# Weight differences over three tiles a chunk, earlier stores of B's pieces, another order of the first chunks, and 128-row low-rank products

## The chip, the cores and the metric

One core of a Trainium2 chip runs the kernel alone. The metric is the device time of one execution in microseconds (us), as the median of the runs of one kernel; lower is better.

## The reference

`x` has 32 sequences of 128 rows and 2048 columns, all in fp32. Each sequence has an adapter number between 6 and 15. The result adds to `x` a linear layer with bias and the low-rank product of the sequence's adapter:

```
result = einsum('bsd,od->bso', x, base_weight) + base_bias     # 2048 x 2048 weights
A, Bw  = lora_A_w[adapter_ids], lora_B_w[adapter_ids]          # rank 16, 32 adapters
h      = einsum('bsd,brd->bsr', x, A)
out    = x + result + einsum('bsr,bor->bso', h, Bw)
```

## The kernel before, in words

**Splitting.** Every fp32 operand is split into a rounded part (hi) and a rest (lo), and a product is three products: hi with hi, lo with hi, hi with lo. ScalarE writes the hi part (`x_high` L544, `w_high` L549), VectorE the lo part (`x_low` L646, `w_low` L651).

**Phases.** The large product is done with seven half-size products in place of eight (the Strassen-Winograd scheme). The seven are the phases P1, P2, P6, P5, P4, P7, P3, in this order. A phase has 16 tiles of 128 rows; a tile has 8 chunks (k) of 128 input columns, and its sums lie in one of two PSUM accumulators, `acc[0]` and `acc[1]`, by turns. Tile number 2i+j of a phase is `Tile(ph, i, j)`; `place` counts the tiles through all phases (P1 has places 0 to 15, P2 has 16 to 31). The first two tiles are written out apart: TensorE takes chunk 0 of both, then chunk 1 of both, and so on, since weights still arrive (L928 to L934).

**Weight differences.** P6, P5, P4 and P7 use differences of blocks of the weights. They are made during P1. For each of 8 chunks, SyncE loads four blocks of 512 KB into the buffers 2 to 5 of `pool` (`prep_load`, L457), GpSimd makes four subtractions (`prep`, L795), and SyncE stores all four to `w_sums` in DRAM (`prep_store`, L463). Chunk i is loaded in the tile (i, 1) and stored one step later.

**B's pieces.** The matrices B of all adapters are split too, in 8 pieces of 512 KB. Piece n is loaded to buffer 6 (`load_piece`), ScalarE and VectorE write its two parts to `b_stack` (`piece_high`, `piece_low`, both in a tile with j = 1), and `store_piece` (L370) writes three times 512 KB of stacked rows to `b_stacks` in DRAM. Piece 0 is the bias, which `spread_bias` copies to all adapters. Pieces 0 to 4 are made in P1, 5 to 8 in P6. The store of a piece stands in the tile pair behind the one that splits it, and `piece_high` of the next piece waits until it has landed.

**Low-rank part.** h of a sequence is a by-product of P1/P2 and P5/P4 (32 more columns of the weights). In P2, P4, P7 and P3, each tile ends with `turn` (L890: a product of `h_cols` with the unit matrix turns h, 50 rows come out) and `low_rank` (L898: these 50 rows of `h_stack` with the 50 rows of `b_stack`: three stacks of 16 and two of bias). TensorE does both inside the next tile, behind its chunks 1 and 2.

**Queues.** Each engine runs a fixed list in order. SyncE (SP) issues every DMA: its list is the function `step` (L468), called for each place in turn. A wait in it holds up all that stands behind it. In `step(place p)` the x block of tile p+2 is loaded (`load_x`, L298), then A's rows (`load_a`), the block to be added (`load_out`), then the weight blocks, pieces and stores in the order of the function. VectorE's step for place p-1 makes the lo part of tile p and reads out tile p-2; TensorE's tile p waits for both.

Of the kernel before, what the change touches and what calls it, by code (L numbers as in the profile page):

```python
# [19 lines left out]
P = 128  # L20
# [4 lines left out]
RANK = 16  # L25
# [36 lines left out]
PREP_AT = (2, 3, 4, 5)  # L62
BUFFERS = 7

# [45 lines left out]
def loads_before(ph):  # L110

    n = [0] * BUFFERS
    for q in range(ph):
        n[0] += PAIRS
        n[1] += PAIRS
        if q == P1:
            for b in PREP_AT:
                n[b] += PAIRS
# [9 lines left out]
def stores_before(ph):  # L128
    n = [0] * BUFFERS
    for q in range(ph):  # L130
        if q == P1:
            for b in PREP_AT:
                n[b] += PAIRS
# [43 lines left out]

def lora_kernel(nc, xT, x, wT, bias, aT, bT, ids, w_sums, s_sums, u4, bias_rows, b_stacks, out):
# [3 lines left out]
    with ctx:  # L182
# [25 lines left out]
        h_cols = at("h_cols", [P, AC + AC], f32r)  # L208
# [35 lines left out]
        bias_spread = sem("bias_spread")  # L244
        out_added = sem("out_added")
# [42 lines left out]
        def _(sp):  # L288
# [53 lines left out]
            def load_b(tile):  # L342
# [99 lines left out]
            def load_w_first(ph):  # L442

                if ph == P6:
                    for b in PREP_AT:
                        sp.wait_ge(pool_out[b], DMA * PAIRS)
# [10 lines left out]
            def prep_load(i):  # L457
                for b, (half, k) in zip(PREP_AT, ((0, 0), (1, 0), (1, KC), (0, KC))):
                    if not (isinstance(i, int) and i == 0):
                        sp.wait_ge(pool_out[b], DMA * i)  # L460
                    sp.dma_start(pool[:, b], wT[half, bass.ds(k + i, 1)]).then_inc(pool_in[b], DMA)  # L461

            def prep_store(i):  # L463
                sp.wait_ge(w_summed, 4 * i + 4)
                for b, which in zip(PREP_AT, (1, 3, 0, 2)):
                    sp.dma_start(w_sums[which, bass.ds(i, 1)], pool[:, b]).then_inc(pool_out[b], DMA)  # L466

            def step(tile):  # L468
# [7 lines left out]
                if ph == P1 and j == 1:  # L476
                    prep_load(i)
# [57 lines left out]
        def _(act):  # L535
# [38 lines left out]
            def h_high(tile):  # L574
# [8 lines left out]
                nc.scalar.activation(h_cols[:].rearrange("p (c r) -> p c r", c=2)[:, :, 0:RANK],  # L583
                                     h.to_broadcast([P, 2, RANK]), COPY).then_inc(h_hi_done, 1)

            def h_out(tile):
# [4 lines left out]
                nc.scalar.activation(h_stack[0:COLS_B], turned[0:COLS_B, 0:ROWS], COPY).then_inc(h_ready, 1)  # L591
# [202 lines left out]
        def _(gp):  # L794
            def prep(i):  # L795

                b11, b12, b22, b21 = PREP_AT
                for b in PREP_AT:
                    gp.wait_ge(pool_in[b], DMA * (i + 1))
                for n, (to, one, two) in enumerate(((b11, b12, b11), (b12, b22, b12), (b22, b22, b11),  # L800
                                                    (b21, b21, b22))):
                    if n:
                        gp.wait_ge(w_summed, 4 * i + n)
                    nc.gpsimd.tensor_tensor(pool[:, to], pool[:, one], pool[:, two],  # L804
                                            ALU.subtract).then_inc(w_summed, 1)
# [18 lines left out]
            def step(tile):  # L824
# [6 lines left out]
                if ph == P1 and j == 1:  # L831
                    prep(i)
# [19 lines left out]
        def _(pe):  # L852
# [37 lines left out]
            def turn(tile):  # L890
# [4 lines left out]
                nc.tensor.matmul(turned[0:COLS_B, 0:ROWS], h_cols[:, 0:COLS_B], eye[:],  # L895
# [88 lines left out]
```

## Time and profile before

| what | us |
|---|---|
| median of 3 runs (1439.85 to 1442.17) | 1441.3 |
| the profiled execution's own time | 1439.74 |
| its span, first to last instruction | 1437.5 |

The span holds the work of all engines; 2.2 us of the execution's time lie around it. TensorE is busy for 1358.2 us of the span, VectorE for 592.6, GpSimd for 255.9, ScalarE for 222.2. In the views PE is TensorE's matmuls, PEld its weight loads, DVE VectorE, ACT ScalarE, POOL GpSimd, SPq SyncE's queue. PEclk and "clock" are the granted TensorE clock: 1.00 or 9 in tenths is 2.4 GHz, and a mean in between is a stretch that was partly at 1.2 GHz. A group in the timeline starts at the first number and takes the second; `[idle before <-releaser]` says how long its engine had stood idle and what ended that.

### The profile page before, as it was taken

How to read it: one execution, taken by the hardware profiler on the slowest of the kernel's cores; microseconds unless marked ns; L12 is line 12 of the kernel's file. 1: busy time of each engine (PE TensorE's matmuls, PEld its weight loads, DVE VectorE, ACT ScalarE, POOL GpSimd, SP SyncE). 2: the span in 40 equal slices, each digit the busy share in tenths (PEclk: the TensorE clock that was granted, in tenths of full speed). 3: DMA queues.
4: the chain of work that ended last, by engine and by line, in shares of the span. 5: the costliest groups of instructions: out<-in, count | busy, mean ns of one | idle time of the engine just before them, and what ended most of it. 6: DMA issues, size and time to landing. Idle time of an engine off the chain costs nothing.

```text
span 1437.5 us, 18259 instructions
## 1 busy us (share of the span) xinstructions
PE 1358.2 (94%) x7136; PEld 1212.2 (84%) x7136; DVE 592.6 (41%) x807; ACT 222.2 (15%) x408; POOL 255.9 (18%) x121
## 2 busy tenths in 40 slices
PE   7899677599999999899999999999999999999998
PEld 7899676499999787779999999999977777777776
DVE  4532233544445544444333464333544444522222
ACT  4010011111112211112111121101211111211110
POOL 1522233421221000002444432221100000000000
PEclk9999888699999999999999999999999999999999
DMA  7566565744455887786666883334467768855552
GB/s 241 181 229 219 208 252 188 269 154 154 151 204 200 290 288 261 285 291 244 252 225 224 293 281 100 115 116 174 159 204 232 232 232 290 290 188 190 192 192 99
DMA packets 93513, 308.78 MB, mean 215 GB/s; under 512 B 10482, under 2 KB 19746, under 8 KB 93474
## 3 DMA queue, kind: packets, MB, share of 16 engines
q1 hardware_dynamic: 93474, 308.35, 61.7%
q8 instruction: 14, 0.23, 0.1%
q14 instruction: 25, 0.20, 0.0%
HBM read 211.82 MB, written 97.01 MB: 215 GB/s over the span
## 4 chain that ended last, share of the span: by engine, by line
PE 71%; DMA 11%; SPq 8%; POOL 5%; DVE 2%; issue 2%; ACT 0%; POOLq 0%; DVEq 0%
PE acc L859 25%; PE acc L872 22%; PE acc L865 20%; POOL pool L804 5%; DMA s_sums<-pool 5%; DMA pool<-wT 4%; PE acc L906 3%; SPq L466 1%; SPq L378 1%; SPq L461 1%; DMA w_raw<-wT 1%; SPq L309 1%; SPq L320 1%; SPq L290 1%; DMA pool<-xT 1%
## 5 line engine op out<-in xcount | busy, mean ns | idle before, releaser
L872 PE MATMUL acc<-w_lo,x_hi 128*128 128x352 f32 (+2 forms) x2304 | 571.5, 347 | 6.8 <-DVE w_lo L651 6.8
L872 PEld LDWEIGHTS acc<-w_lo,x_hi 128*128 128x128 f32 x2304 | 408.7, 191 | 41.2 <-DVE w_lo L651 7.4
L859 PE MATMUL acc<-w_hi,x_hi 128*128 128x352 f32 x1536 | 344.4, 333 | 59.1 <-DVE keep L728 40.8
L859 PE MATMUL acc<-w_hi,x_lo 128*128 128x352 f32 x1536 | 336.3, 327 | 0.0
L859 PEld LDWEIGHTS acc<-w_hi,x_hi 128*128 128x128 f32 x1536 | 261.4, 193 | 68.0 <-issue 48.7
L859 PEld LDWEIGHTS acc<-w_hi,x_lo 128*128 128x128 f32 x1536 | 268.6, 192 | 0.0
L865 PE MATMUL acc<-w_hi,x_hi 128*128 128x512 f32 x768 | 246.3, 401 | 5.2 <-DVE x_lo L646 5.1
L865 PE MATMUL acc<-w_hi,x_lo 128*128 128x512 f32 x768 | 241.0, 394 | 0.0
L646 DVE TENSOR_TENSOR x_lo<-pool,x_hi 128x1024 fp32r<-128x1024 f32 x110 | 146.7, 1334 | 204.6 <-ACT x_hi L544 204.6
L544 ACT ACTIVATE x_hi<-pool 128x1024 fp32r<-128x1024 f32 x110 | 116.1, 1056 | 682.7 <-PE acc L872 354.1
L815 POOL TENSOR_TENSOR pool<-pool,keep 128x1024 f32<-128x1024 f32 x48 | 120.5, 2526 | 434.8 <-DMA pool<-x 434.8
L865 PEld LDWEIGHTS acc<-w_hi,x_hi 128*128 128x128 f32 x768 | 139.3, 189 | 50.7 <-issue 9.8
L734 DVE TENSOR_TENSOR pool<-acc,pool 128x352 f32<-128x352 f32 (+2 forms) x176 | 102.2, 631 | 181.8 <-PE acc L906 181.8
L865 PEld LDWEIGHTS acc<-w_hi,x_lo 128*128 128x128 f32 x768 | 144.8, 189 | 33.7
L804 POOL TENSOR_TENSOR pool<-pool 128x1024 f32<-128x1024 f32 x32 | 87.6, 2737 | 184.1 <-DMA pool<-wT 182.2
L651 DVE TENSOR_TENSOR w_lo<-w_raw,w_hi 128x1024 fp32r<-128x1024 f32 x56 | 77.2, 1393 | 41.7 <-ACT w_hi L549 41.3
L690 DVE TENSOR_TENSOR h_sum<-acc,h_part 128x32 f32<-128x32 f32 x32 | 6.1, 192 | 165.7 <-PE acc L872 165.7
L659 DVE TENSOR_TENSOR w_hi<-a_raw,w_hi 128x64 fp32r<-128x64 f32 (+1 forms) x96 | 66.8, 722 | 2.3 <-ACT w_hi L562 2.3
L549 ACT ACTIVATE w_hi<-w_raw 128x1024 fp32r<-128x1024 f32 x56 | 58.2, 1051 | 52.4 <-DMA w_raw<-wT 36.0
L583 ACT ACTIVATE h_cols<-h_keep 128x32 fp32r<-128x32 f32 x64 | 14.3, 223 | 306.8 <-DVE h_keep L693 306.8
L906 PE MATMUL acc<-b_stack,h_stack 50*128 50x512 f32 (+2 forms) x160 | 46.5, 386 | 2.8 <-ACT h_stack L591 2.8
L706 DVE TENSOR_TENSOR keep<-acc,keep 128x1024 f32<-128x1024 f32 x16 | 19.6, 1224 | 67.1 <-PE acc L872 67.1
(29 smaller groups left out, 344.3 us busy)
## 6 DMA issues: line engine op xcount, KB each, us to landing
pool<-xT SPq DMA_DIRECT2D x142, 512.0 KB, 5.8
pool<-x SPq DMA_DIRECT2D x64, 512.0 KB, 5.4
out<-pool SPq DMA_DIRECT2D x48, 512.0 KB, 2.8
pool<-wT SPq DMA_DIRECT2D x32, 512.0 KB, 8.0
w_sums<-pool SPq DMA_DIRECT2D x32, 512.0 KB, 4.0
w_raw<-w_sums SPq DMA_DIRECT2D x32, 512.0 KB, 6.1
s_sums<-pool SPq DMA_DIRECT2D x32, 512.0 KB, 8.8
pool<-s_sums SPq DMA_DIRECT2D x32, 512.0 KB, 5.5
```

What stands on the lines that cost most here:

```text
L544: nc.scalar.activation(x_hi[:, j], x_raw(j), COPY).then_inc(x_hi_done, 1)
L549: nc.scalar.activation(w_hi[:, s, AC:AC + HALF], w_raw[:, s], COPY).then_inc(w_hi_done, 1)
L646: nc.vector.tensor_tensor(x_lo[:, j], x_raw(j), x_hi[:, j], ALU.subtract).then_inc(x_lo_done, 1)
L651: nc.vector.tensor_tensor(w_lo[:, s], w_raw[:, s], w_hi[:, s, AC:AC + HALF], ALU.subtract).then_inc(w_lo_done, 1)
L659: did = nc.vector.tensor_tensor(w_hi[:, s:s + m, hi + RANK:hi + AC], a_raw[:, j, k:k + m], w_hi[:, s:s + m, hi:hi + RANK], ALU.subtract)
L734: did = nc.vector.tensor_tensor(rows, sums, rows, ALU.add)
L804: nc.gpsimd.tensor_tensor(pool[:, to], pool[:, one], pool[:, two], ALU.subtract).then_inc(w_summed, 1)
L815: did = nc.gpsimd.tensor_tensor(to, pool[:, b], kept, ALU.add)
L859: mm = nc.tensor.matmul(acc[j][:, o, 0:COLS_A], xs, w_hi[:, s, base + o * COLS_A:base + (o + 1) * COLS_A], start=(k == 0 and part == 0), s ...
L865: mm = nc.tensor.matmul(acc[j][:, o], xs, w_hi[:, s, AC + o * BANK:AC + (o + 1) * BANK], start=(k == 0 and part == 0), stop=False)
L872: mm = nc.tensor.matmul(acc[j][:, o, low:low + n], x_hi[:, j, k], w_lo[:, slot(ph, k), first:first + n], start=False, stop=end and (ph not ...
L906: mm = nc.tensor.matmul(acc[j][:, o, low:low + m], h_stack[0:COLS_B], b_stack[0:COLS_B, j, first:first + m], start=False, stop=True, skip_ ...
```

## The change

Five things. The differences are made with three buffers (2, 3, 4): three loads, three subtractions and three stores, and then one load, one subtraction and one store in buffer 2 again. A chunk is spread over three tiles (places 4+3n, 5+3n, 6+3n), so that the work runs from place 4 to place 27, into P2. A piece of B is stored in the tile that splits it (j = 1). The first two tiles share their chunks 0 to 4 only; then tile 0 does its last three chunks, then tile 1. `h_cols` has 128 columns, zero beyond the 50, and `turn` and `low_rank` work on 128 rows; for this GpSimd clears the rows of `b_stack` once in P1 and once in P6 (`clear_b`), and the first `load_b` of P2 and of P4 waits for it.

```diff
-PREP_AT = (2, 3, 4, 5)
+PREP_AT = (2, 3, 4)
+PREP_FROM = 4
+FIRST_CHUNKS = [(j, k) for k in range(5) for j in range(2)] + [(j, k) for j in range(2) for k in range(5, KC)]
...
+def prep_at(tile):
+    n, part = divmod(place(tile) - PREP_FROM, 3)
+    return (n, part) if 0 <= n < KC else (None, None)
...
-        h_cols = at("h_cols", [P, AC + AC], f32r)
+        h_cols = at("h_cols", [P, P], f32r)
...
-                if n < 2:
-                    sp.wait_ge(piece_out, DMA * (2 + 3 * 4))
-                elif ph == P4 and i == 0:
-                    sp.wait_ge(piece_out, DMA * (2 + 3 * 8))
+                if i == 0 and ph in (P2, P4):
+                    sp.wait_ge(b_cleared, 1 if ph == P2 else 2)
...
-            def prep_load(i):
-                for b, (half, k) in zip(PREP_AT, ((0, 0), (1, 0), (1, KC), (0, KC))):
-                    if not (isinstance(i, int) and i == 0):
-                        sp.wait_ge(pool_out[b], DMA * i)
-                    sp.dma_start(pool[:, b], wT[half, bass.ds(k + i, 1)]).then_inc(pool_in[b], DMA)
-
-            def prep_store(i):
-                sp.wait_ge(w_summed, 4 * i + 4)
-                for b, which in zip(PREP_AT, (1, 3, 0, 2)):
-                    sp.dma_start(w_sums[which, bass.ds(i, 1)], pool[:, b]).then_inc(pool_out[b], DMA)
+            def prep_load(n):
+                a, b, c = PREP_AT
+                if n:
+                    sp.wait_ge(pool_out[a], DMA * 2 * n)
+                    sp.wait_ge(pool_out[b], DMA * n)
+                    sp.wait_ge(pool_out[c], DMA * n)
+                for at, what in ((a, wT[0, n]), (b, wT[1, n]), (c, wT[1, KC + n])):
+                    sp.dma_start(pool[:, at], what).then_inc(pool_in[at], DMA)
+
+            def prep_store(n):
+                a, b, c = PREP_AT
+                sp.wait_ge(w_summed, 4 * n + 3)
+                for at, which in ((a, 1), (b, 3), (c, 0)):
+                    sp.dma_start(w_sums[which, n], pool[:, at]).then_inc(pool_out[at], DMA)
+
+            def prep_load_last(n):
+                a = PREP_AT[0]
+                sp.wait_ge(pool_out[a], DMA * (2 * n + 1))
+                sp.dma_start(pool[:, a], wT[0, KC + n]).then_inc(pool_in[a], DMA)
+
+            def prep_store_last(n):
+                a = PREP_AT[0]
+                sp.wait_ge(w_summed, 4 * n + 4)
+                sp.dma_start(w_sums[2, n], pool[:, a]).then_inc(pool_out[a], DMA)
...
-                if ph == P1 and j == 1:
-                    prep_load(i)
+                chunk, part = prep_at(tile)
+                if part == 0:
+                    prep_load(chunk)
+                if part == 2:
+                    prep_load_last(chunk)
...
-                if j == 0 and (place(tile) - 2) // 2 in range(PAIRS):
-                    prep_store((place(tile) - 2) // 2)
-                if j == 0 and i > 0 and piece_at(Tile(ph, i - 1, 0)) is not None:
-                    store_piece(piece_at(Tile(ph, i - 1, 0)))
+                if part == 1:
+                    prep_store(chunk)
+                if part == 2:
+                    prep_store_last(chunk)
+                if j == 1 and piece_at(tile) is not None:
+                    store_piece(piece_at(tile))
...
-                nc.scalar.activation(h_stack[0:COLS_B], turned[0:COLS_B, 0:ROWS], COPY).then_inc(h_ready, 1)
+                nc.scalar.activation(h_stack[:], turned[:, 0:ROWS], COPY).then_inc(h_ready, 1)
...
+            def clear_b(pieces):
+                gp.wait_ge(piece_out, DMA * (3 * pieces - 1))
+                nc.gpsimd.memset(b_stack[:].bitcast(f32), 0.0).then_inc(b_cleared, 1)
...
-                nc.tensor.matmul(turned[0:COLS_B, 0:ROWS], h_cols[:, 0:COLS_B], eye[:],
+                nc.tensor.matmul(turned[:, 0:ROWS], h_cols[:], eye[:],
...
-                    mm = nc.tensor.matmul(acc[j][:, o, low:low + m], h_stack[0:COLS_B], b_stack[0:COLS_B, j, first:first + m],
+                    mm = nc.tensor.matmul(acc[j][:, o, low:low + m], h_stack[:], b_stack[:, j, first:first + m],
...
-            for k in range(KC):
-                for j in range(2):
+            for j, k in FIRST_CHUNKS:
```

GpSimd's `prep` and `prep_last` make the same four subtractions, each with a wait for the blocks that it reads. Which instruction stands where in SyncE's list is seen in its rows. Before, in P1 from the store of a chunk's four differences on (place 8): the three stores of a piece of B (L378) stand behind the four stores (L466), then tile 10's block of x (L309) and A's rows, and in the next step the first of the next chunk's four loads (L461).

```order
L466 DMA w_sums<-pool 128x1024 [waits w_summed]
L466 DMA w_sums<-pool 128x1024 x3
L378 DMA b_stacks<-b_stack 8x16x1024 [waits piece_split]
L378 DMA b_stacks<-b_stack 8x16x1024 x2
L309 DMA pool<-xT 128x1024 [waits x_lo_done]
L290 TENSOR_LOAD ids_sb
L290 ISA x2
L339 ISA [waits a_ready]
L339 DMA a_raw<-aT 128x128
L461 DMA pool<-wT 128x1024 [waits pool_out2]
```

Now, the places 7 and 8, which load chunk 1's three blocks (L474) and store its first three differences (L480); L388 is the store of a piece, L321 the load of x, L378 the load of the next piece:

```order
L474 DMA pool<-wT 128x1024 [waits pool_out4,pool_out3,pool_out2]
L474 DMA pool<-wT 128x1024 x2
L388 DMA b_stacks<-b_stack 8x16x1024 [waits piece_split]
L388 DMA b_stacks<-b_stack 8x16x1024 x2
L321 DMA pool<-xT 128x1024 [waits x_lo_done]
L302 TENSOR_LOAD ids_sb
L302 ISA x2
L351 ISA [waits a_ready]
L351 DMA a_raw<-aT 128x128
L378 DMA pool<-bT 128x1024 [waits piece_split]
L480 DMA w_sums<-pool 128x1024 [waits w_summed]
L480 DMA w_sums<-pool 128x1024 x2
```

And place 9, with the fourth block (load L485, store L490) and a piece's stores:

```order
L321 DMA pool<-xT 128x1024 [waits x_lo_done]
L302 TENSOR_LOAD ids_sb
L302 ISA x2
L351 ISA [waits a_ready]
L351 DMA a_raw<-aT 128x128
L485 DMA pool<-wT 128x1024 [waits pool_out2]
L490 DMA w_sums<-pool 128x1024 [waits w_summed]
L388 DMA b_stacks<-b_stack 8x16x1024 [waits piece_split]
L388 DMA b_stacks<-b_stack 8x16x1024 x2
```

Three blocks of x are now loaded for a chunk's eight transfers, where two were before; but SyncE waits for GpSimd twice a chunk (L480, L490), and for a landed store twice (L485, L474).

TensorE, at the end of the first two tiles, from chunk 5 on. Before, the tiles take turns:

```order
L859 MATMUL acc0<-w_hi_49,x_hi_52 128x352 x3
L859 MATMUL acc0<-w_hi_49,x_lo_53 128x352 x3
L872 MATMUL acc0<-w_lo_50,x_hi_52 128x320
L872 MATMUL acc0<-w_lo_50,x_hi_52 128x352 x2
L859 MATMUL acc1<-w_hi_49,x_hi_52 128x352 x3
L859 MATMUL acc1<-w_hi_49,x_lo_53 128x352 x3
L872 MATMUL acc1<-w_lo_50,x_hi_52 128x352 x2
L872 MATMUL acc1<-w_lo_50,x_hi_52 128x320
```

Now tile 0 (`acc0`) goes on with chunk 6, and the three last chunks of tile 1 stand at the end:

```order
L905 MATMUL acc0<-w_hi_49,x_hi_52 128x352 x3
L905 MATMUL acc0<-w_hi_49,x_lo_53 128x352 x3
L918 MATMUL acc0<-w_lo_50,x_hi_52 128x320
L918 MATMUL acc0<-w_lo_50,x_hi_52 128x352 x2
L905 MATMUL acc0<-w_hi_49,x_hi_52 128x352 x3
L905 MATMUL acc0<-w_hi_49,x_lo_53 128x352 x3
L918 MATMUL acc0<-w_lo_50,x_hi_52 128x320
L918 MATMUL acc0<-w_lo_50,x_hi_52 128x352 x2
```

Tile 0's last matmul thus stands three chunks of tile 1 before the end of the pair, in place of one.

## Rows read from the trace of the kernel before

**Rows 1.** The page's slices of 36 us: TensorE's granted clock in tenths

```profile
PEclk9999888699999999999999999999999999999999
```

**Rows 2.** A window (PE, PEld, DVE, ACT, POOL busy; clock; DMA share; GB/s)

```profile
150.00:180.00 30.00, 18.61 (x101) 18.64 (x102) 8.93 (x13) 3.46 (x5) 10.42 (x4) 0.77 0.58 210
```

**Rows 3.** Waits of TensorE, 0 to 300 us: total, times, longest

```profile
PE acc L859 <- DVE keep L728: 40.8, 6, 11.5
PE acc L859 <- ACT w_hi L549: 18.4, 2, 10.5
PE acc L872 <- DVE w_lo L651: 6.8, 1, 6.8
```

**Rows 4.** Timeline of SyncE's queue, one chunk of differences with B's stores

```profile
137.08 2.87 SPq L466 DMA_DIRECT2D w_sums<-pool  x4
139.99 5.60 SPq L378 DMA_DIRECT2D b_stacks<-b_stack  x3
...
149.79 4.00 SPq L461 DMA_DIRECT2D pool<-wT  x4
...
173.02 2.86 SPq L466 DMA_DIRECT2D w_sums<-pool  x4
```

**Rows 5.** Timeline of the other engines in that cycle

```profile
156.95 1.04 ACT L544 ACTIVATE x_hi<-pool 128x1024 fp32r<-128x1024 f32 x1
162.34 10.65 POOL L804 TENSOR_TENSOR pool<-pool 128x1024 f32<-128x1024 f32 x4 [25.29 <-DMA pool<-wT]
```

**Rows 6.** Timeline of TensorE, its restart after that stall

```profile
161.39 1.22 PE L859 MATMUL acc<-w_hi,x_hi 128*128 128x352 f32 x3 [11.47 <-DVE keep L728]
...
168.31 0.65 PE L859 MATMUL acc<-w_hi,x_hi 128*128 128x352 f32 x3
```

**Rows 7.** Timeline: a chunk of differences without B's stores

```profile
245.83 2.87 SPq L466 DMA_DIRECT2D w_sums<-pool  x4
...
261.46 12.30 POOL L804 TENSOR_TENSOR pool<-pool 128x1024 f32<-128x1024 f32 x4 [15.65 <-DMA pool<-wT]
```

**Rows 8.** Timeline of ScalarE: the starts of tiles 3 and 7

```profile
53.81 1.06 ACT L544 ACTIVATE x_hi<-pool 128x1024 fp32r<-128x1024 f32 x1 [18.88 <-PE acc L872]
...
99.84 1.06 ACT L544 ACTIVATE x_hi<-pool 128x1024 fp32r<-128x1024 f32 x1 [10.21 <-PE acc L872]
```

**Rows 9.** Timeline: TensorE around the end of tile 1, VectorE at the end of P2's first tile

```profile
32.95 0.63 PE L872 MATMUL acc<-w_lo,x_hi 128*128 128x352 f32 x3
...
40.24 1.22 PE L859 MATMUL acc<-w_hi,x_hi 128*128 128x352 f32 x3 [6.65 <-DVE keep L728]
...
281.20 0.19 DVE L690 TENSOR_TENSOR h_sum<-acc,h_part 128x32 f32<-128x32 f32 x1 [1.43 <-PE acc L872]
```

**Rows 10.** DMA part of the page: median us from issue to landing

```profile
pool<-wT SPq DMA_DIRECT2D x32, 512.0 KB, 8.0
w_sums<-pool SPq DMA_DIRECT2D x32, 512.0 KB, 4.0
```

**Rows 11.** Timeline of TensorE in P3 around a low-rank product (L906)

```profile
1241.74 0.63 PE L872 MATMUL acc<-w_lo,x_hi 128*128 128x512 f32 x2
1242.30 0.73 PE L906 MATMUL acc<-b_stack,h_stack 50*128 50x512 f32 x2
1242.96 0.73 PE L865 MATMUL acc<-w_hi,x_hi 128*128 128x512 f32 x2
1243.53 0.64 PE L865 MATMUL acc<-w_hi,x_lo 128*128 128x512 f32 x2
```

**Rows 12.** The same stretch: TensorE's weight loads

```profile
1242.30 0.29 PEld L906 LDWEIGHTS acc<-b_stack,h_stack 50*128 50x128 f32 x2 [0.37 <-issue]
1242.96 0.30 PEld L865 LDWEIGHTS acc<-w_hi,x_hi 128*128 128x128 f32 x2 [0.36 <-ACT w_hi L549]
1243.30 0.42 PEld L865 LDWEIGHTS acc<-w_hi,x_lo 128*128 128x128 f32 x2
```

**Rows 13.** Waits of TensorE, 440 to 700 us (P6 and P5's begin)

```profile
PE acc L865 <- DVE x_lo L646: 5.1, 3, 4.0
```

More of the change, by code:

```diff
@@ L116, in loads_before @@
         if q == P1:
-            for b in PREP_AT:
-                n[b] += PAIRS
+            for b, times in zip(PREP_AT, (2, 1, 1)):
+                n[b] += times * KC
         n[B_AT] += len(PIECE_IN.get(q, ()))
@@ L131, in stores_before @@
         if q == P1:
-            for b in PREP_AT:
-                n[b] += PAIRS
+            for b, times in zip(PREP_AT, (2, 1, 1)):
+                n[b] += times * KC
         if q == P6:
@@ L244, in lora_kernel @@
         bias_spread = sem("bias_spread")
+        b_cleared = sem("b_cleared")
         out_added = sem("out_added")
@@ L445, in load_w_first @@
                     for b in PREP_AT:
-                        sp.wait_ge(pool_out[b], DMA * PAIRS)
+                        sp.wait_ge(pool_out[b], DMA * STORES[P2][b])
                 if ph >= 2:
@@ L794, in _, with prep, prep_last @@
         def _(gp):
[L795 to L805, printed above, removed]
+            def prep(n):
+                a, b, c = PREP_AT
+                gp.wait_ge(pool_in[a], DMA * (2 * n + 1))
+                gp.wait_ge(pool_in[b], DMA * (n + 1))
+                nc.gpsimd.tensor_tensor(pool[:, a], pool[:, b], pool[:, a], ALU.subtract).then_inc(w_summed, 1)
+                gp.wait_ge(pool_in[c], DMA * (n + 1))
+                gp.wait_ge(w_summed, 4 * n + 1)
+                nc.gpsimd.tensor_tensor(pool[:, b], pool[:, c], pool[:, b], ALU.subtract).then_inc(w_summed, 1)
+                gp.wait_ge(w_summed, 4 * n + 2)
+                nc.gpsimd.tensor_tensor(pool[:, c], pool[:, c], pool[:, a], ALU.subtract).then_inc(w_summed, 1)
+            def prep_last(n):
+                a, _, c = PREP_AT
+                gp.wait_ge(pool_in[a], DMA * (2 * n + 2))
+                gp.wait_ge(w_summed, 4 * n + 3)
+                nc.gpsimd.tensor_tensor(pool[:, a], pool[:, a], pool[:, c], ALU.subtract).then_inc(w_summed, 1)
+            def clear_b(pieces):
+                gp.wait_ge(piece_out, DMA * (3 * pieces - 1))
+                nc.gpsimd.memset(b_stack[:].bitcast(f32), 0.0).then_inc(b_cleared, 1)
             def add_out(tile):
@@ L830, in step @@
                     add_out(tile)
-                if ph == P1 and j == 1:
-                    prep(i)
+                chunk, part = prep_at(tile)
+                if part == 0:
+                    prep(chunk)
+                if part == 2:
+                    prep_last(chunk)
+                if ph in PIECE_IN and i == PAIRS - 1 and j == 0:
+                    clear_b(PIECE_IN[ph][-1] + 1)
             nc.gpsimd.memset(eye_raw, 0.0).then_inc(eye_filled, 1)
@@ L926, in whole @@
                         low_rank(back)
-            for k in range(KC):
-                for j in range(2):
-                    if k == 0:
-                        pe.wait_ge(a_ready, j + 1)
-                    if k % 2 == 0:
-                        pe.wait_ge(first_lo, k + j + 1)
-                    chunk(Tile(P1, 0, j), k)
+            for j, k in FIRST_CHUNKS:
+                if k == 0:
+                    pe.wait_ge(a_ready, j + 1)
+                if k % 2 == 0:
+                    pe.wait_ge(first_lo, k + j + 1)
+                chunk(Tile(P1, 0, j), k)
             for ph in PHASES:
```

2 lines of the change are left out of this document (1 added, 1 removed).

## The prediction

> **What bounds the kernel now.** I read the page's slices first. The clock row is at 9 everywhere but in four slices, from about 144 to 288 us [rows 1]. From the window inside them the reader is to see that TensorE is busy for 18.6 of 30 us, with a mean clock of 0.77, while the DMA engines work for 58% of it and GpSimd for a third [rows 2]: nobody is full, so a chain of waits sets the pace. Next the waits of TensorE in the first 300 us: 40.8 + 18.4 + 6.8 = 66.0 us, most of them for the readout of an earlier tile [rows 3]. Outside this stretch the list is short (5.1 us around P6 [rows 13]), so P1 is where waiting can be removed, and elsewhere only TensorE's own work counts.
>
> Why P1 waits is read in SyncE's queue. Four stores of differences go out at 137.08, three stores of a piece of B behind them, a block of x, and only at 149.79 the next chunk's four loads [rows 4]. GpSimd waits 25.29 us, begins at 162.34 and needs 10.65 [rows 5]; SyncE waits for all four, and its next stores go out at 173.02 [rows 4]. The cycle takes 35.9 us. It covers two tiles, and a tile that is not held up takes (99.84 - 53.81) / 4 = 11.5 us [rows 8]. So each chunk of this kind costs TensorE some 12.9 us, because the blocks of x stand in the same queue behind those waits.
>
> **How much there is to gain in P1.** Tile 1 ends at 33.6 (its last group starts at 32.95 and takes 0.63), and P2's first tile at 281.2 [rows 9]. Between them lie 15 tiles, 172.5 us without a wait. They would end at 206.1: the most that P1 can give is 75.1 us, the 66.0 of waits and the time at 1.2 GHz behind each of them. One such restart: three chunks from 161.39 to 168.31 take 6.9 us [rows 6] in place of 3 x 11.5 / 8 = 4.3, so 2.6 are lost.
>
> **First tiles.** Tile 2 can't be made ready before tile 0 is summed. Tile 0 ended one chunk (1.4 us) before the pair's end, and TensorE waited 6.65 us for tile 2's operands and tile 0's readout [rows 9]. Now it ends three chunks, 4.3 us, before. From a block of x that is there to the start of its tile ScalarE and VectorE need 161.39 - 156.95 = 4.4 us [rows 5, 6], as 4.3 are given. GpSimd, whose subtractions began then, has nothing until place 4. Tile 2 starts at 33.6 to 33.8 in place of 40.24; with the restart saved, tile 3 starts near 45.1, not 53.8 [rows 8]. This is part of the 75.1.
>
> **The new queue in P1.** I follow SyncE's list with a price for each transfer. Without B's stores, from the first of four stores to GpSimd's begin it takes 15.6 us for nine blocks of 512 KB [rows 7]: 1 us to start and 1.6 a block. With B's three, 162.34 - 137.08 = 25.3 [rows 4, 5], so one of B's costs 9.7 / 3 = 3.2. The critical transfer is tile 14's block of x. Ahead of it, from place 4 on, stand eight blocks of x, 11 loads and 11 stores of differences, four loads of pieces, P2's first four weight blocks: 39 with itself, 62 us; four times three stores of B, 38; A's rows and the spread bias, 5. Together 105. SyncE comes to place 4 when piece 0 is split, 5 us into tile 3, and is through with its stores at 51.5. With a queue that is never empty the block lands at 157. It is needed 4.4 us before 171.6, at 167. But the queue does run empty: at each wait for GpSimd, who needs 2.7 us for a subtraction (10.65 / 4 [rows 5]), about 5 us at the first wait of a chunk and 4 at the second, and where SyncE, ahead of TensorE at places 5 and 6, waits for x_lo and the split of piece 1. I count 20 us. The block lands at 177: **10 us late**, 2.6 for the restart, and about 4 more where P2's last four weight blocks stand behind place 15's waits. P1 keeps 17 of the 75, so **the gain is 58**. Bounds: 75, if nothing is late, and 35, if the lateness is 25 and comes in two stalls more.
>
> **P2.** Four of the eight chunks now lie here. A chunk's chain is three loads (8.0 to land), three subtractions (8.0), the first store (4.0), the load in its buffer (8.0), a subtraction (2.7), the store (4.0) [rows 5, 10]: 34.7 us. It has three tiles, so TensorE's own 11.5 [rows 8] and some 0.6 each for its two low-rank instructions: 36.2 us. SyncE's wait for a readout lies beside this chain, and 17 blocks at 1.6 are 27 us. I cost it at nothing; the cover is 1.5 us a chunk, and if the chain has 40 us, four chunks cost 15.
>
> **Low-rank products.** In P3, groups of two 128x512 matmuls start 0.46 us apart. Around `low_rank` it is 0.56, 0.66 and 0.57 (1241.74 to 1243.53) [rows 11]: 0.40 us more than three groups cost. The weight loads show why: before the 50-row load PEld stands idle for 0.37 us, and before the first 128-row load behind it for 0.36, while each other load begins under the matmuls ahead of it [rows 12]. With 128 rows throughout, both breaks should go: 64 low-rank products x 0.39 = 25 us, all of it on TensorE's path, as the phases P2, P4, P7 and P3 have it busy without a break. `turn` loads 128 columns, not 50, under other work; I take 1 us for that, with 0 and 4 as ends (0.07 each). **Gain 24**, with 0 as the lower end.
>
> The Trainium skill speaks against it: "TensorE: Matmul & The Clock Gate", Part 3, says that a weight load overlaps matmuls in flight only when its row group differs. By that rule a 128-row load would overlap nothing, the edit would give 0 and the sum below would be 24 us longer; the trace, where 128-row loads run under 128-row matmuls, does not agree.
>
> **The rest.** B's stores in P6 move half a tile pair ahead; DMA is the bound there for some tiles [rows 13], and I take 0, with -3 and +6. The two clears of `b_stack` are GpSimd's, which has nothing else to do then: 0. The last tile is as before.
>
> **Sum**, against the execution of 1439.7 (1437.5 of span and 2.2 around): 1439.7 - 58 - 24 = 1357.7. The median stands 1.6 higher, so the forecast is **1359**.
>
> **The rivals.**
> 1. *P1 has no wait left.* For it: with the queue full the block lands 10 us early, and I estimated the empty stretches. Against it: every chunk has two waits for GpSimd. 1441.3 - 75 - 25 = 1341.
> 2. *SyncE's chain stays the bound longer.* P1 keeps 26 and P2's chunks take 40 us: 9 + 15 more, 1383. For it: 1.5 us of cover in P2 is little.
> 3. *128 rows give nothing*, since the two breaks come from the waits that `low_rank` has, not from its rows: 1383. Against it: the second break stands before an ordinary product, and `turn`, which waits too, has none.
> 4. *Slower: the waits add up instead of lying side by side.* In P1 a chunk would take 39.4 us (loads 9, subtractions 8, store 5.3, load 9.1, subtraction 2.7, store 5.3) and B's stores 9.6; in P2 the same 39.4 and three waits for a readout of 6.2. Eight chunks: 4 x 49 + 4 x 58 = 428 us, where TensorE needs 12 x 11.5 + 12 x 12.1 = 283 and 7 are there in reserve. That loses 138 where the kernel before lost 75; with 24 back it gives 1441 + 63 - 24 = 1480. It decides from 48.6 us a chunk on, (283 + 7 + 75 + 24) / 8. Against it: the loads of a chunk and SyncE's other work do overlap in the queue.
>
> The order of the instructions shows that the change does what it says, so that is no rival.
>
> **How the numbers follow.** Forecast 0.58, rival 1 0.17, rival 2 0.11, rival 3 0.10, rival 4 0.04. From 1339 to 1388 the first four are held, with P6's ends; what is outside is rival 4 and the ends of the second and third taken together. A measurement of this kernel can't tell less than 0.2%, 2.9 us, from no change. Faster 0.96; of rival 4's 0.04 a quarter may end within 0.2%.
>
> **What would show it.** The profile after should have P2's first tile end near 223; TensorE without a wait until about 170 us and then one stall of some 10 us before tile 14; no clock below 9 before that; the tiles of P3 0.39 us closer to each other than before; PEld without idle time at L906's successor; the four chunks of P2 without a wait of TensorE. An end of P2's first tile beyond 240, or groups of two matmuls that still start 0.56 to 0.66 us apart around `low_rank`, would make it wrong.

## The result, and the profile after

The changed kernel takes 1356.8 us (median of 4 runs, 1353.05 to 1361.67), the kernel before 1440.6 on the same chip: a ratio of 0.9422, interval 0.9387 to 0.9458. It is faster, and the forecast of 1359 is 2.2 us off. The profiled execution was the slowest of the four, 1361.67, with a span of 1359.9; stage times below are differences within such profiled spans. Medians and ratios count the fast executions alone; a slow one of the kernel with the spread and the earlier store, 2521.92 us at a granted clock of 0.904, is left out.

The slices of the page of the changed kernel, which answer to [rows 1], and its busy times:

```profile
PE 1321.9 (97%) x7136; PEld 1209.9 (89%) x7136; DVE 574.5 (42%) x807; ACT 222.1 (16%) x408; POOL 255.5 (19%) x123
...
PEclk9999989999999999999999999999999999999999
```

One slice, near 170 to 200 us, is left of the four below 9. ScalarE's operation that writes `x_hi` of a given place (`x_high`) marks where a stage begins; the time between two such marks is that of the stage:

| stage (places) | before, us | after, us | gained | forecast |
|---|---|---|---|---|
| P1 and P2's first tiles (to place 18) | 281.8 | 220.7 | 61.1 | 58 |
| rest of P2 (18 to 32) | 178.1 | 179.4 | -1.3 | 5.5 |
| P6 | 187.6 | 187.7 | -0.1 | 0 |
| P5 | 183.7 | 183.7 | 0.0 | 0 |
| P4 | 203.8 | 198.2 | 5.6 | 6.2 |
| P7 | 193.5 | 188.0 | 5.5 | 6.2 |
| P3 and the end | 209.1 | 202.3 | 6.8 | 6.2 |

(The forecast for the low-rank part is 16 products a phase x 0.39 us.) P1 gave 61 of the 78 us of span, the phases with low-rank products the rest; only P2 gave nothing.

The waits of TensorE in the first 300 us of the changed kernel, where [rows 3] had 66 us (columns: who waited, for whose output, us, times, longest):

```profile
PE acc L905 <- DVE keep L757: 9.3, 1, 9.3
PE acc L905 <- ACT w_hi L578: 8.0, 1, 8.0
PE turned L941 <- DVE h_cols L728: 3.6, 3, 2.1
```

Where they lie is read in TensorE's timeline:

```profile
8.03 1.22 PE L905 MATMUL acc<-w_hi,x_hi 128*128 128x352 f32 x3 [8.03 <-ACT w_hi L578]
181.41 1.22 PE L905 MATMUL acc<-w_hi,x_hi 128*128 128x352 f32 x3 [9.35 <-DVE keep L757]
```

The wait of 8.0 us is the start of the program, before TensorE's first matmul; the kernel before has it too, with 7.84 us, inside the 18.4 of [rows 3]. The wait of 9.3 is the stall that was forecast before tile 14. From 181.41 on TensorE runs without a wait to the end of P2's first tile: "about 4 more" for P2's last weight blocks didn't come. The third wait is new. The window that answers to [rows 2] (columns: stretch, its length, busy time of PE, PEld, DVE, ACT and POOL, granted clock, DMA share, GB/s):

```profile
150.00:180.00 30.00, 22.06 (x139) 21.79 (x137) 8.78 (x11) 3.67 (x6) 4.34 (x2) 0.96 0.61 212
```

The stall is read in ScalarE's row for tile 14 and in SyncE's queue (timeline of the changed kernel; [4.00 <-DMA] is ScalarE's idle time and what ended it):

```profile
175.04 1.06 ACT L573 ACTIVATE x_hi<-pool 128x1024 fp32r<-128x1024 f32 x1 [4.00 <-DMA pool<-xT]
```

```profile
151.31 1.63 SPq L480 DMA_DIRECT2D w_sums<-pool  x3
152.99 5.20 SPq L388 DMA_DIRECT2D b_stacks<-b_stack  x3
158.23 6.31 SPq L450 DMA_DIRECT2D w_raw<-wT  x4
164.59 1.03 SPq L321 DMA_DIRECT2D pool<-xT  x1
```

Ahead of tile 14's block of x (L321, issued at 164.59) stand B's stores and P2's first four weight blocks, as in the forecast's list. ScalarE took it at 175.04; the forecast had it landed at 177.

**What went wrong in P2** is read around 257 us. The changed kernel's timeline, GpSimd, VectorE and TensorE together:

```profile
256.68 2.39 POOL L829 TENSOR_TENSOR pool<-pool 128x1024 f32<-128x1024 f32 x1 [0.21 <-DMA pool<-wT]
257.00 2.10 DVE L722 TENSOR_TENSOR h_keep<-h_sum 128x16 f32<-128x16 f32 x1
259.21 2.35 POOL L832 TENSOR_TENSOR pool<-pool 128x1024 f32<-128x1024 f32 x1
259.40 2.19 DVE L728 TENSOR_TENSOR h_cols<-h_keep,h_cols 128x16 fp32r<-128x16 f32 x1 [0.30 <-ACT h_cols L612]
261.72 0.32 PE L941 MATMUL turned<-eye,h_cols 128*128 128x128 f32 x1 [2.11 <-DVE h_cols L728]
263.93 1.05 PE L952 MATMUL acc<-b_stack,h_stack 128*128 128x352 f32 x3
264.78 1.08 PE L905 MATMUL acc<-w_hi,x_hi 128*128 128x352 f32 x3
```

Two operations of VectorE on 16 columns take 2.10 and 2.19 us. Each ends within 0.1 us of the subtraction of GpSimd beside it. TensorE waits 2.11 us for the second. Its groups of three behind it take up to 1.08 us, where such a group takes 0.65 at full clock; the granted clock of this stretch is 0.91, and the seven groups behind `turn` take 4.92 us, where they take 3.39 behind the `turn` at 223.08, which had waited 1.30 us:

```profile
260.00:280.00 20.00, 18.28 (x105) 18.29 (x106) 12.04 (x16) 2.63 (x9) 7.23 (x3) 0.91 0.59 197
```

Without an operation of GpSimd beside it the first takes 0.17:

```profile
272.96 0.17 DVE L722 TENSOR_TENSOR h_keep<-h_sum 128x16 f32<-128x16 f32 x1
```

In P2 the second operation is late five times, at 220.84, 259.40, 297.59, 335.36 and 360.60. In four of them the first one was late too (1.39, 2.10, 1.23 and 0.78 us), and there TensorE waits 1.30, 2.11, 1.27 and 0.66 us; at 297.59 the first took its usual time, and the wait is about 0.1. So the slack of one chunk covers one late operation, but not two in a row, and two in a row come where GpSimd has several operations back to back. Over the whole of P2, the durations of the second operation (minimum/median/maximum in ns), the changed kernel's first and the kernel before's second:

```profile
L728 DVE TENSOR_TENSOR h_cols<-h_keep,h_cols x15: 174/176/2279, 220.8 to 397.5; 128x16 fp32r<-128x16 f32 x15
```

```profile
L699 DVE TENSOR_TENSOR h_cols<-h_keep,h_cols x14: 174/175/176, 295.3 to 457.2; 128x16 fp32r<-128x16 f32 x14
```

Before, GpSimd had no subtractions of weights in P2, and none of the 14 was late. But the same thing stood in the trace of the kernel before, in P4, where GpSimd adds blocks. Twelve small operations took 1.58 to 2.36 us there, one a tile, and TensorE waited for `h_cols` only 0.5 us in all. GpSimd's row and VectorE's, in the kernel before:

```profile
879.67 2.40 POOL L815 TENSOR_TENSOR keep<-pool,keep 128x1024 f32<-128x1024 f32 x1 [1.73 <-DMA pool<-x]
879.92 2.19 DVE L699 TENSOR_TENSOR h_cols<-h_keep,h_cols 128x16 fp32r<-128x16 f32 x1 [0.29 <-ACT h_cols L583]
```

The windows of P2, after and then before, show what was moved in: GpSimd's busy time goes from 37 to 76 us.

```profile
220.00:400.00 180.00, 174.37 (x1080) 172.72 (x1079) 81.22 (x133) 27.66 (x74) 75.61 (x31) 0.99 0.75 254
```

```profile
281.00:460.00 179.00, 179.00 (x1089) 172.60 (x1088) 78.08 (x134) 27.61 (x75) 37.39 (x14) 0.99 0.48 166
```

The Trainium skill bears on it: its page "GPSIMD Engine Reference" says that GpSimd shares its SBUF interface with VectorE, with contention when VectorE's instruction has two inputs in SBUF. The rows agree: both operations read two SBUF tensors and take 2.1 us in place of 0.17, while `h_sum` (L719), with one input in PSUM, takes 0.18 to 0.19 us all 32 times, at 218.93 too, where GpSimd works beside it.

Last, P3, where [rows 11, 12] had the two breaks around `low_rank`. TensorE's groups and the weight loads of one tile of the changed kernel:

```profile
1193.97 0.62 PE L918 MATMUL acc<-w_lo,x_hi 128*128 128x512 f32 x2
1194.43 0.63 PE L952 MATMUL acc<-b_stack,h_stack 128*128 128x512 f32 x2
1194.90 0.62 PE L911 MATMUL acc<-w_hi,x_hi 128*128 128x512 f32 x2
```

```profile
1193.74 0.42 PEld L918 LDWEIGHTS acc<-w_lo,x_hi 128*128 128x128 f32 x2
1194.20 0.42 PEld L952 LDWEIGHTS acc<-b_stack,h_stack 128*128 128x128 f32 x2
1194.67 0.42 PEld L911 LDWEIGHTS acc<-w_hi,x_hi 128*128 128x128 f32 x2
```

The groups start 0.46 and 0.47 us apart (before 0.56 and 0.66), and each load begins 0.04 or 0.05 us behind the one before it. Both breaks are gone.

### The profile page after: what moved, and what is told of

Same layout as the page of the kernel before. It is cut to its first block, busy times and chain, and to the rows that moved or that the text cites. A ratio compares the mean times of both kernels' runs of the same rounds, so it can differ in the third digit from the quotient of the medians.

```text
span 1359.9 us, 18276 instructions
## 1 busy us (share of the span) xinstructions
PE 1321.9 (97%) x7136; PEld 1209.9 (89%) x7136; DVE 574.5 (42%) x807; ACT 222.1 (16%) x408; POOL 255.5 (19%) x123
## 4 chain that ended last, share of the span: by engine, by line
PE 76%; DMA 12%; SPq 5%; DVE 4%; POOL 2%; issue 1%; ACT 1%; POOLq 0%; DVEq 0%; ACTq 0%
PE acc L905 30%; PE acc L918 24%; PE acc L911 20%; DMA s_sums<-pool 7%; PE acc L952 2%; DMA pool<-wT 2%; DMA pool<-xT 2%; DVE h_keep L722 1%; SPq L332 1%; DVE h_cols L728 1%; SPq L388 1%; SPq L340 1%; PE turned L941 1%; SPq L321 1%; SPq L450 0%
## 5 line engine op out<-in xcount | busy, mean ns | idle before, releaser
L918 PEld LDWEIGHTS acc<-w_lo,x_hi 128*128 128x128 f32 x2304 | 404.4, 189 | 33.3
L905 PE MATMUL acc<-w_hi,x_hi 128*128 128x352 f32 x1536 | 336.4, 328 | 17.4 <-DVE keep L757 9.3
L905 PE MATMUL acc<-w_hi,x_lo 128*128 128x352 f32 x1536 | 332.2, 324 | 0.0
L675 DVE TENSOR_TENSOR x_lo<-pool,x_hi 128x1024 fp32r<-128x1024 f32 x110 | 137.9, 1254 | 222.0 <-ACT x_hi L573 221.9
L680 DVE TENSOR_TENSOR w_lo<-w_raw,w_hi 128x1024 fp32r<-128x1024 f32 x56 | 70.5, 1274 | 45.9 <-ACT w_hi L578 45.6
L719 DVE TENSOR_TENSOR h_sum<-acc,h_part 128x32 f32<-128x32 f32 x32 | 6.2, 192 | 148.8 <-PE acc L918 148.8
L704 DVE TENSOR_TENSOR pool<-pool 128x1024 f32<-128x1024 f32 x16 | 19.6, 1226 | 90.4 <-DMA pool<-xT 90.4
L688 DVE TENSOR_TENSOR w_hi<-a_raw,w_hi 128x64 fp32r<-128x64 f32 (+1 forms) x96 | 47.3, 520 | 2.1 <-ACT w_hi L591 2.1
L856 POOL TENSOR_TENSOR keep<-pool,keep 128x1024 f32<-128x1024 f32 x16 | 40.5, 2533 | 37.9 <-DMA pool<-x 37.1
```

The costliest lines, as they stand in the source:

```text
L675: nc.vector.tensor_tensor(x_lo[:, j], x_raw(j), x_hi[:, j], ALU.subtract).then_inc(x_lo_done, 1)
L680: nc.vector.tensor_tensor(w_lo[:, s], w_raw[:, s], w_hi[:, s, AC:AC + HALF], ALU.subtract).then_inc(w_lo_done, 1)
L688: did = nc.vector.tensor_tensor(w_hi[:, s:s + m, hi + RANK:hi + AC], a_raw[:, j, k:k + m], w_hi[:, s:s + m, hi:hi + RANK], ALU.subtract)
L704: nc.vector.tensor_tensor(pool[:, s1], pool[:, j], pool[:, s1], ALU.add).then_inc(x_summed, 1)
L856: did = nc.gpsimd.tensor_tensor(to, pool[:, b], kept, ALU.add)
L905: mm = nc.tensor.matmul(acc[j][:, o, 0:COLS_A], xs, w_hi[:, s, base + o * COLS_A:base + (o + 1) * COLS_A], start=(k == 0 and part == 0), s ...
```

## The experiments

The rivals were tried by parts: 128 rows alone, the first chunks alone, the spread alone, and then by single edits of the changed kernel for what was left of its waits. In the lists of waits the one of 8 to 9 us for `w_hi` is the program's start each time. Ratios are to the kernel before, which took 1439.1 to 1439.6 us beside them. "First P2 tile" is the mark of place 18; in the changed kernel it is at 220.7.

### 128 rows alone

```diff
-        h_cols = at("h_cols", [P, AC + AC], f32r)
+        h_cols = at("h_cols", [P, P], f32r)
...
-                nc.tensor.matmul(turned[0:COLS_B, 0:ROWS], h_cols[:, 0:COLS_B], eye[:],
+                nc.tensor.matmul(turned[:, 0:ROWS], h_cols[:], eye[:],
...
-                    mm = nc.tensor.matmul(acc[j][:, o, low:low + m], h_stack[0:COLS_B], b_stack[0:COLS_B, j, first:first + m],
+                    mm = nc.tensor.matmul(acc[j][:, o, low:low + m], h_stack[:], b_stack[:, j, first:first + m],
```

> The kernel before with the 128-row low-rank products alone (128 columns of h_cols, the clears of b_stack). Theory (the breaks come from the 50 rows): 64 x 0.39 = 25 us less 1 for turn, so about 1416 us, and groups of two matmuls 0.46 us apart around the low-rank product in P3. Rival (the breaks come from the waits of low_rank): no change, 1440, and breaks of 0.56 to 0.66 us remain.

Measured: 1414.98 us (1411.81 to 1416.68), ratio 0.9826 (0.9811 to 0.9841): 24 us gained, as forecast. Beside the lines shown, the kernel has the clears of `b_stack` and ScalarE's copy of 128 rows. TensorE in P3 of this kernel:

```profile
1237.28 0.62 PE L877 MATMUL acc<-w_lo,x_hi 128*128 128x512 f32 x2
1237.74 0.63 PE L911 MATMUL acc<-b_stack,h_stack 128*128 128x512 f32 x2
1238.21 0.62 PE L870 MATMUL acc<-w_hi,x_hi 128*128 128x512 f32 x2
```

Rival 3 falls: `low_rank`'s waits are still there, its breaks are not. What made the breaks is the number of rows. The rule of the Trainium skill quoted in the prediction ("TensorE: Matmul & The Clock Gate", Part 3) doesn't hold here: loads of the same 128 rows overlap the matmuls ahead of them. The same Part of the Trainium skill also lets a load into the background weight buffer run ahead; whether this is one, no row shows. The Trainium skill's other page that bears on it, "TensorEngine Tiling (Array Packing)", Key Properties, says that a change of the tiling mode drains TensorE. Whether 50 rows between 128 are such a change that page doesn't say; the trace fits it, with about 0.4 us for the way to 50 rows and back (24.15 us by 64 products are 0.38).

### The first chunks alone

```diff
-            for k in range(KC):
-                for j in range(2):
...
+            for j, k in FIRST_CHUNKS:
```

> The kernel before with the new order of the first two tiles' chunks alone. My sum counted its 8.7 us inside P1's 75. Theory (P1's pace is set by SyncE's list and the queue from 44 us on): tile 3 may start earlier, but P2's first tile ends at 279 to 281 as before, and the time is within 2 us of 1440. Rival (the gain is TensorE's own): 8.7 us less, 1432.

Measured: 1439.01 us, ratio 0.9999 (0.9990 to 1.0009). P2's first tile is summed at 279.64 in place of 281.20 [rows 9]. While SyncE's chain bounds P1, an earlier tile 2 only waits longer later: the 6.65 us before tile 2 are gone, and a stall of 2.39 us at 125 has become one of 9.14 at 123.

### The spread alone, and with the earlier store

Both are the kernel before with the differences over three tiles. The second has the earlier store of B's pieces as well:

```diff
-                if j == 0 and i > 0 and piece_at(Tile(ph, i - 1, 0)) is not None:
-                    store_piece(piece_at(Tile(ph, i - 1, 0)))
+                if j == 1 and piece_at(tile) is not None:
+                    store_piece(piece_at(tile))
```

> The kernel before with the differences spread over three tiles a chunk and three buffers alone (B's stores one pair later, old first chunks, 50 rows). Theory: most of P1's gain is this part's, since SyncE's list no longer holds x back behind four subtractions: 45 to 60 us less, 1380 to 1395. Rival (B's stores or the first tiles carry it): less than 30 us.

> The same, and B's pieces stored in the tile that splits them. Theory: the store moves half a pair ahead and so out of the busiest stretch before tile 14: 3 to 10 us less than with the spread alone. Rival (the number of bytes counts, not their place): the same within 2 us.

Measured: the spread alone 1381.83 us (1380.06 to 1383.8), ratio 0.9604 (0.9589 to 0.9619), 57 us gained. With the earlier store 1385.71 (1384.03 to 1390.58), ratio 0.9641 (0.9617 to 0.9664). The waits of TensorE in the first 230 us, first without the earlier store, then with it:

```profile
PE acc L905 <- ACT w_hi L580: 8.7, 2, 8.0
PE acc L905 <- DVE keep L759: 7.0, 2, 4.1
```

```profile
PE acc L905 <- DVE keep L759: 12.0, 2, 9.1
PE acc L905 <- ACT w_hi L580: 9.0, 1, 9.0
```

The spread alone makes as much as the whole change in P1 (first P2 tile at 220.5 from 281.8, in the changed kernel 220.7; there the new first chunks and the earlier store cancel). The earlier store was expected to give 3 to 10 us; the medians stand 4 us apart the other way, with intervals that touch. The wait for the readout grows from 7.0 to 12.0 us, and all of that is one stall: 4.15 us before tile 15 has become 9.12 before tile 14. The last piece's three stores, issued at 172.07 behind tile 14's block of x, are now issued at 157.87, ahead of it (169.50). Neither theory had that. One more us of the difference is the program's start, 8.02 and 9.02 us in these two executions.

### The changed kernel with the first chunks of before

```diff
-            for j, k in FIRST_CHUNKS:
...
+            for k in range(KC):
+                for j in range(2):
```

> The changed kernel with the old order of the first chunks. GpSimd has nothing to do there now, so tile 2 loses 3 us of operands' latency and the restart: tiles 2 to 11 start 3 to 5 us later. Theory (SyncE's list is late by then at tile 14 anyway and starts from piece 0's split, which moves along): the time is 2 to 5 us longer. Rival (the queue's lateness at tile 14 absorbs it): the same within 2 us.

Measured: 1361.91 us (1359.93 to 1365.06), ratio 0.9461 (0.9447 to 0.9476). Against the changed kernel's 1356.8 it is 5 us more, and P2's first tile is 3.5 us later. The same edit that was worth nothing alone is worth some us once the queue no longer bounds all of P1.

### The turn after chunk 3

```diff
-TURN_AFTER, LORA_AFTER = 1, 2
+TURN_AFTER, LORA_AFTER = 3, 4
```

> The changed kernel with turn and low_rank behind chunks 3 and 4 in place of 1 and 2. Theory (in P2 VectorE's small operations on h wait for GpSimd's subtractions, 2.1 us in place of 0.17, and TensorE waits at turn and falls to 1.2 GHz): the wait of turn for h_cols (7.0 us) goes, P2's 14 tiles from 220.7 on take 169 to 172 us in place of 179.4, and the time falls by 5 to 9 us to about 1349. Rival (the later readout makes SyncE's wait for acc_read longer, and x and the stores late): no change or slower by some us.

Measured: 1347.61 us (1346.02 to 1348.9), ratio 0.9359 (0.9345 to 0.9373), 9 us below the changed kernel. P2 from place 18 to 32 takes 171.9 us, not 179.4, and P4 194.1, not 198.2. The waits of TensorE, whole span:

```profile
PE acc L905 <- DVE keep L757: 9.3, 1, 9.3
PE acc L905 <- ACT w_hi L578: 8.0, 1, 8.0
PE acc L911 <- DVE x_lo L675: 5.9, 4, 3.2
PE acc L952 <- ACT h_stack L620: 1.8, 2, 1.4
```

The wait for `h_cols`, 7.0 us in 11 times in the changed kernel, is no longer in the list. VectorE's operation is still late in P2 of this kernel:

```profile
L728 DVE TENSOR_TENSOR h_cols<-h_keep,h_cols x4: 176/176/2056, 256.3 to 291.5; 128x16 fp32r<-128x16 f32 x4
```

Now it lies under two more chunks of TensorE. So the wait at `turn` and what TensorE lost behind it were P2's loss. (Of P4's 4 us, the waits at `turn` were 1.5; the rest was not followed.) How much it is differs with where the subtractions fall: between the same marks P2 took 172.6 us with 128 rows alone (no subtractions there), 171.9 to 173.4 in the three kernels with the late turn, and 173.0 to 180.1 in the five with subtractions and the turn after chunk 1.

### Tile 14's block of x ahead of P2's weights

```diff
+                    if tile == Tile(P1, PEELED, 0):
+                        load_w_first(P2)
...
-                if ph + 1 < len(PHASES):
+                if P1 < ph and ph + 1 < len(PHASES):
```

`load_w_first(P2)` now stands behind `load_x` of tile 14.

> The changed kernel with tile 14's block of x issued ahead of P2's first four weight blocks at place 12 in place of behind them. Theory (the stall of 9.3 us before tile 14 is this block behind four stores' worth of queue): the block is issued 6.3 us earlier, the stall falls to about 3 to 4 us, and the time by 5 to 8 us. Rival (the chain of differences sets the pace, and x only shows it): the stall comes back one tile later, at tile 15 or 16, and the time is the same.

Measured: 1354.81 us (1352.1 to 1358.33), ratio 0.9419 (0.9403 to 0.9435). The wait for the readout falls from 9.3 to 5.7 us and P2's first tile comes at 217.6, so the blocks did hold it up; of 3 us gained there the whole time shows 2, which is inside the changed kernel's own interval. The expected 5 to 8 was too much: the last piece's stores are still ahead of the block, and now P2's weights come later and cost 1.1 us at 209.59.

### The stores of B on another queue, and one pair later

The first lets ScalarE's queue store pieces 1 to 8, and one tile pair later as well; the second puts the store back where the kernel before had it:

```diff
-                if j == 1 and piece_at(tile) is not None:
-                    store_piece(piece_at(tile))
...
+                act.wait_ge(piece_split, n + 1)
...
+                    act.dma_start(b_stacks[8 * q:8 * q + 8, half, first:first + RANK],
+                                  b_stack[:, part].bitcast(f32)).then_inc(piece_out, DMA)
```

```diff
-                if j == 1 and piece_at(tile) is not None:
-                    store_piece(piece_at(tile))
+                if j == 0 and i > 0 and piece_at(Tile(ph, i - 1, 0)) is not None:
+                    store_piece(piece_at(Tile(ph, i - 1, 0)))
```

> The changed kernel with the stores of B's pieces 1 to 8 issued by ScalarE on its own queue, in the first tile of the next pair, in place of SyncE. Theory (what delays x in P1 is standing behind B's stores in one list and one queue): the stall before tile 14 goes and P1 ends 5 to 12 us earlier. Rival (the DMA engines' bytes set it, whoever issues them): the same within 3 us, or slower, as ScalarE is held up while it issues.

> The changed kernel with B's pieces stored one tile pair later, as in the kernel before. Theory (e4 against e3: the early store stands in front of x at place 11, and costs 4 to 6 us): 2 to 6 us less than the changed kernel, 1351 to 1355. Rival (with the other parts in place the early store is what keeps it out of the stretch of P2's first weights): slower by 2 to 5 us.

Measured: on ScalarE's queue 1369.54 us (1369.17 to 1372.17), ratio 0.9518 (0.9504 to 0.9533), 13 us slower than the changed kernel. Its waits, whole span, without the program's start:

```profile
PE acc L914 <- DVE x_lo L678: 16.6, 5, 4.4
PE acc L908 <- DVE keep L760: 9.7, 1, 9.7
```

The wait for the readout stays at 9.7. ScalarE's queue sends the last piece's stores at 150.18, so they still run ahead of tile 14's block of x, which stands behind P2's weights in SyncE's list (157.11 to 165.12). Another queue alone doesn't take them out of its way. In P6 it costs. The windows of P6 in this kernel and then in the changed one:

```profile
395.00:600.00 205.00, 186.53 (x791) 149.94 (x791) 92.66 (x85) 29.72 (x32) 4.20 (x2) 0.97 0.76 263
```

```profile
400.00:588.00 188.00, 179.73 (x782) 145.52 (x781) 88.93 (x82) 29.41 (x32) 4.22 (x2) 0.99 0.81 285
```

P6 takes 202.5 us between its marks in place of 187.7; with the same later place and SyncE's queue (the next kernel) it takes 185.2, so the later place alone doesn't cost it. The lower rate, 263 GB/s in place of 285, is the same bytes over the longer time and explains nothing by itself. Why P6 is longer was not tried further.

One pair later: 1354.28 us (1349.49 to 1355.83), ratio 0.9402 (0.9386 to 0.9418), 2.5 less than the changed kernel, and inside its interval. The wait for the readout falls from 9.3 to 1.8, P2's first tile comes 7 us earlier, at 213.8. Tile 14's block of x is issued here at 151.48, and the last piece's stores come behind it:

```profile
151.48 0.54 SPq L321 DMA_DIRECT2D pool<-xT  x1
```

The 1.8 us are before tile 15. In P2's first tile TensorE waits 2.95 us for weights at 205.89. P2 then takes 180.1, and TensorE waits at `turn` 10 times for 7.3 us.

### The edits that helped, together

One kernel has the turn after chunk 3, tile 14's block first and B's store one pair later. A second one also starts the chunks one place later and lets P6's first weights wait for the stores of one buffer alone:

```diff
-PREP_FROM = 4
+PREP_FROM = 5
...
-                    for b in PREP_AT:
-                        sp.wait_ge(pool_out[b], DMA * STORES[P2][b])
+                    b = PREP_AT[2]
+                    sp.wait_ge(pool_out[b], DMA * STORES[P2][b])
```

> The changed kernel with the later turn and low_rank, the later store of B's pieces, and tile 14's x ahead of P2's first weights. If the three gains of 9, 2 and 2 to 6 us lie at different waits they add up: 1339 to 1345. If the last two lie at the same wait before tile 14, one of them goes: 1343 to 1347.

> The same with the differences begun one place later (place 5, so 5 to 28), and P6's first weights waiting only for the differences that P6 reads. Theory (the wait of 8.0 us in P2's first tile is P2's last four weight blocks standing behind the wait for chunk 3's subtractions at place 14): at place 15 the weights now stand ahead of that wait, the 8.0 us fall to 2 or less, 1334 to 1340. Rival (SyncE is late by then anyway, and the weights' own way through the queue takes as long): the wait stays at 6 to 8 us and the time is that of the run before within 3 us.

Measured: 1346.07 us (1342.61 to 1348.2), ratio 0.9346 (0.9332 to 0.9359), and 1346.12 (1343.81 to 1348.72), ratio 0.9349 (0.9335 to 0.9363). Both are 11 us below the changed kernel, 93 below the one before; they can't be told from the late turn alone (1347.6). The gains of the single edits, 9 + 2 + 2.5, don't add up; two of them lie at the same stall before tile 14. The waits that are left in P1 and P2's first tiles, of the first kernel and then of the second:

```profile
PE acc L907 <- ACT w_hi L580: 9.9, 2, 8.6
PE acc L907 <- DVE keep L759: 4.1, 1, 4.1
```

```profile
PE acc L907 <- ACT w_hi L580: 7.9, 1, 7.9
PE acc L907 <- DVE keep L759: 2.7, 1, 2.7
```

The second kernel was built against a wait of 8.0 us for `w_hi` in P2's first tile, and there is none: that wait is the program's start (8.60 and 7.89 us in these two). What the first kernel has in P2's first tile is 1.26 us at 208.69. In the second one P2's later four weight blocks are issued at 189.99 (in the changed kernel at 202.18, and its P2 begins 6 us later), and this wait is gone. The stall, in these two before tile 15, falls from 4.1 to 2.7, and P2's first tile comes 2 us earlier, at 214.6; the whole time doesn't show it.

## Why the prediction was right

**P1's gain of 58.** The marks give 61.1, the spread alone 61.3. Most of its steps held: no wait between the program's start and the stall; one stall of 9.35 us (10 forecast) before tile 14, from a block that ScalarE took at 175.0 (177 forecast). Behind the stall three chunks take 7.15 us in place of 4.3, so 2.9 are lost (2.6 forecast). The step that failed is the last one, "about 4 more" for P2's last four weight blocks: TensorE waits for none of them, and that term is 0. P2's first tile is summed at 218.93 (223 forecast), 12.8 behind the bound of 206.1, and 9.35 and 2.9 make 12.2 of it:

```profile
218.93 0.19 DVE L719 TENSOR_TENSOR h_sum<-acc,h_part 128x32 f32<-128x32 f32 x1 [1.72 <-PE acc L918]
```

The 20 us of empty queue were an estimate by count, with rival 1 at none of them, so that it came within 2 us of the landing is in part luck. The bound of 75.1 stands, but what it is made of was misread: of the 66.0 us of waits 7.84 are the program's start, before tile 1's end, so 58.2 are waits inside it and 17 the time at 1.2 GHz.

**First tiles, 8.7 us of P1's 75.** The early gain is there: TensorE starts tile 2 at 33.75 without a wait (33.6 to 33.8 forecast), and tile 3's start, when ScalarE takes tile 4's block, is at 45.55 in place of 53.81 [rows 8] (45.1 forecast). At the end of P1 3.5 us of it are left, and 5 in the whole time; alone it is worth nothing, since the queue then takes it back. TensorE's row and ScalarE's:

```profile
33.75 0.72 PE L905 MATMUL acc<-w_hi,x_hi 128*128 128x352 f32 x3
45.55 1.06 ACT L573 ACTIVATE x_hi<-pool 128x1024 fp32r<-128x1024 f32 x1 [10.48 <-PE acc L918]
```

**B's stores earlier.** They were taken as part of P1's queue, priced by their bytes (38 us) wherever they stand. Their place counts too: in two pairs of kernels the earlier place is 4 and 2.5 us slower, each about as much as can be told, and in both P1's wait for the readout is longer by it (7.0 to 12.0, 1.8 to 9.3), since the last piece's stores then run ahead of tile 14's block.

**P2 at nothing.** This step failed. The chain of differences costs TensorE nothing, as forecast: behind 220 us it waits in P2 for `h_cols` alone. What was missed lies elsewhere: GpSimd's subtractions run beside VectorE's small operations of the low-rank part, and these had only one chunk of slack. The prediction had no term for it, though P4 of the kernel before shows such operations at 2 us. P2 took 1.3 us more where its low-rank products should have given 5.5, so 6.8 us were lost: 5.5 of waits and 1.5 at the lower clock make 7.0. With the late turn P2 takes 7.5 less. The forecast's sign for P2, that its chunks would be without a wait of TensorE, was wrong for this reason:

```profile
PE turned L941 <- DVE h_cols L728: 5.5, 5, 2.1
```

**Low-rank products, 24.** Measured alone: 24 us, 5.5 of them in P2. In the changed kernel P4, P7 and P3 give 5.6, 5.5 and 6.8, with 6.2 forecast for each, and P2's share went into the loss above.

**P6's 0 and the clears' 0.** P6 takes 187.7 us in place of 187.6. Right.

The sum came out within 2.2 us because errors cancel: P1 gave 3 us more, P2 7 less, and that this ends near the forecast is luck. The profiled execution, whose stages are counted here, also stands 5 us above the median, so that any of these stages may be off by a few us. The rivals: 1 (no wait left, 1341) asked for 75 in P1, which no kernel here reached, the best having 68 with the store late; 2 (chain of 40 us) shows no sign; 3 is refuted by 128 rows alone; 4 (slower) by the time itself.

## What to carry to other kernels

A chain of load, compute and store that holds up a queue costs what stands behind it; spread it over more tiles until the engine's own pace covers it, and then look at what stands ahead of the next critical block. When work of GpSimd is moved under another phase, count the small operations of VectorE that run beside it and the slack of whoever waits for them; a phase where the two already meet shows the price. And look up where in time a wait lies before building against it: a list of waits doesn't tell the program's start from a stall. And keep the rows of all matmuls in a row equal, if zeros can fill them: a product of fewer rows may cost more than a full one.

## What the runs showed of the hardware

- An operation of VectorE on 128x16 values with two inputs in SBUF took up to 2.4 us, not 0.17, beside GpSimd's operation on 128x1024 values, and ended with it, in the changed kernel's P2 and in P4 of the kernel before. With one input in PSUM it took its usual 0.19.
- A 50-row low-rank product between 128-row ones costs about 0.4 us of TensorE's time in this kernel; with 128 rows, 24 us in 64 products went away.
- With the stores of B's pieces one pair later on ScalarE's queue P6 took 202.5 us, one pair later on SyncE's 185.2. The cause is not shown.
- A store of a piece of B (8x16x1024) costs 3.2 us of the queue, where a block of the same size costs 1.6, an estimate from [rows 4, 5, 7]. The Trainium skill, "DMA: Bandwidth & Descriptors", "How many engines (k)", says that the outermost dimension decides how many engines share a transfer; 8 there against 16 engines would give the factor of two of this estimate. No row here shows the number of engines.
